# Delta-rule stage: output product one place later, norms' product at the end of the odd place, other orders on the engines

## What is computed

```python
q = _l2norm(q) * DK ** (-0.5); k = _l2norm(k)      # after a causal convolution and silu
def step(S, xs):
    q_t, k_t, v_t, g_t, b_t = xs
    S = S * jnp.exp(g_t)[..., None, None]
    kv = jnp.einsum('bhk,bhkv->bhv', k_t, S)
    S = S + jnp.einsum('bhk,bhv->bhkv', k_t, (v_t - kv) * b_t[..., None])
    o_t = jnp.einsum('bhk,bhkv->bhv', q_t, S)
    return (S, o_t)
o = o * jax.lax.rsqrt(mean(o * o) + EPS) * norm_w * jax.nn.silu(z)
return o.reshape(b_, t_, V_DIM) @ W_out
```

## Time and profile before

| | us |
|---|---|
| median of 3 runs | 2767.0 (2761.95 to 2785.57) |
| the profiled execution, its own time | 2778.46 |
| its span (first to last instruction) | 2776.8 |
| TensorE busy in the span | 2194.6 (79%) |
| VectorE busy | 1890.6 (68%) |
| ScalarE busy | 1435.8 (52%) |
| GpSimd busy | 769.1 (28%) |

### The profile page before, as it was taken

One profiled execution on the slowest core, in us unless ns is written; L12 is line 12 of the kernel. 1 busy time (PEld: TensorE's weight loads), 2 busy tenths in 40 slices (PEclk: granted clock), 3 DMA queues, 4 the chain that ended last, 5 costly groups with the idle time before them and its releaser, 6 DMA issues. The chain is left out here.

```text
span 2776.8 us, 63709 instructions
## 1 busy us (share of the span) xinstructions
PE 2194.6 (79%) x25656; PEld 1388.4 (50%) x25656; DVE 1890.6 (68%) x4429; ACT 1435.8 (52%) x2901; POOL 769.1 (28%) x845
## 2 busy tenths in 40 slices
PE   2698888889888493468888888888888886587984
PEld 1244444444444282146666666666666664365552
DVE  2477677777766325568888898888888883673433
ACT  0376667667666221255666666666666644132321
POOL 1000001000010141024444444344444442202884
PEclk8599899999887796668888988888888888597997
DMA  5000000000000042200000000000000000433334
GB/s 187 26 1 5 5 5 9 5 5 8 5 7 6 25 117 53 65 9 11 12 12 12 12 12 12 12 12 11 11 12 12 4 4 6 139 110 91 53 43 86
DMA packets 109526, 85.53 MB, mean 31 GB/s; under 512 B 22366, under 2 KB 97282, under 8 KB 108976
## 3 DMA queue, kind: packets, MB, share of 16 engines
q1 hardware_dynamic: 95664, 68.31, 8.4%
q0 software_dynamic: 13568, 13.14, 2.9%
HBM read 59.22 MB, written 22.71 MB: 30 GB/s over the span
## 5 line engine op out<-in xcount | busy, mean ns | idle before, releaser
L617 ACT ACTIVATE Pr<-Pr,nmax 128x512 f32<-128x512 f32 x512 | 341.2, 714 | 177.4 <-DVE nmax L552 175.3
L722 PE MATMUL bank<-ident,Pr 128*128 128x128 f32 x2048 | 315.5, 297 | 71.6 <-DVE PT L561 59.8
L722 PEld LDWEIGHTS bank<-ident,Pr 128*128 128x128 f32 x2048 | 242.1, 151 | 258.8 <-DVE PT L561 157.2
L552 DVE CUSTOM_DVE_ANT_0 Pr<-bank,Tb 128x512 f32<-128x512 f32 x512 | 331.0, 684 | 42.4 <-PE bank L708 42.3
L561 DVE COPY PT<-bank 128x512 f32<-128x512 f32 x256 | 176.4, 689 | 188.2 <-PE bank L736 184.0
L2431 PE MATMUL bank<-Wcv,hw 128*128 128x512 f32 x512 | 265.1, 665 | 8.8 <-POOL hw L1985 5.3
L2173 DVE TENSOR_TENSOR pr<-AC,Tc 128x30 f32<-128x30 f32 (+14 forms) x480 | 214.9, 448 | 16.9 <-POOL Tc L2049 3.6
L624 ACT ACTIVATE PT<-bank 128x512 f32<-128x512 f32 x256 | 151.0, 590 | 112.9 <-PE bank L736 83.3
L2174 DVE TENSOR_TENSOR Tc<-Tc,pr 128x30 f32<-128x30 f32 (+14 forms) x480 | 178.8, 373 | 16.5
L708 PE MATMUL bank<-kp,qp 8*128 8x512 f32 x1024 | 178.4, 696 | 1.1 <-DVE nmax L552 1.1
L2431 PEld LDWEIGHTS bank<-Wcv,hw 128*128 128x128 f32 x512 | 103.5, 214 | 125.8 <-issue 118.0
(11 more groups left out here) (398 smaller groups left out, 4533.6 us busy)
## 6 DMA issues: line engine op xcount, KB each, us to landing
aB<-alpha SPq DMA_DIRECT2D x64, 128.0 KB, 2.7
Tb<-scores SPq DMA_DIRECT2D x1, 7168.0 KB
w<-in_L_ffn_W SPq DMA_DIRECT2D x16, 256.0 KB, 5.2
rawW<-in_L_ffn_up_w SPq DMA_DIRECT2D x16, 256.0 KB, 3.1
rawW<-in_L_ffn_gw SPq DMA_DIRECT2D x16, 256.0 KB, 3.5
rawW<-in_L_ffn_down_w SPq DMA_DIRECT2D x16, 256.0 KB, 4.0
disp<-zero SPq DMA_DIRECT2D x1, 2580.0 KB, 15.5
xin<-disp SPq DMA_DIRECT2D x8, 322.5 KB, 6.3
```

What stands on the lines that cost most here:

```text
L552: V.tensor_tensor_reduce(out=Pr[:, s, i, :], in0=pS[hh][:, :], in1=Tb[:, h, at:at + L], scale=-1.0, scalar=3.0e38, op0=ALU.add, op1=ALU.mi ...
L617: A_(Pr[:, s, i, :], Pr[:, s, i, :], ACT.Exp, scale=-1.0, bias=nmax[:, s, i:i + 1])\
L722: last = TR(pT[m % 2][:, t * P:(t + 1) * P], Pr[:, (G % 2) * HG + hh, t, j * P:(j + 1) * P], ident[:, :])
```

## The change

On TensorE the output product of step k-1 moves from the end of place k to place k+1, behind the first project; the loop has one place more. The norms' product of a pair moves from the even place, behind read_out, to the end of the odd place ahead of it, behind turned. add_state(k,1) moves behind keys and gate(k,0). MISC follows. ScalarE: output one place later, behind the first project; roots from the middle of the even place to the end of the odd one; in even places weights(k,0) behind the second project. VectorE: norms(m+1) ahead of the first conv; inverse_norm right behind the second conv in both places; no substitution ahead of accumulate(k,0) in the odd place, rows 18 to 23 ahead of accumulate(k,1). GpSimd: decay(k,0) ahead of the first diag, weigh(k,0) ahead of the second. SP: the output's DMA one place later.

```diff
-            FIRST, LAST = -4, NS + 1
+            FIRST, LAST = -4, NS + 2
 (MISC)
-                if k % 2 == 0 and 0 <= k // 2 + 1 < NP:
-                    MISC += [("nm", k // 2 + 1)]
+                if 0 <= k - 2 < NS:
+                    MISC += [("out", k - 2)]
...
-                    MISC += [("ot", 2 * (k - 1)), ("ot", 2 * (k - 1) + 1), ("out", k - 1)]
+                    MISC += [("ot", 2 * (k - 1)), ("ot", 2 * (k - 1) + 1)]
+                if k % 2 == 1 and 0 <= k // 2 + 2 < NP:
+                    MISC += [("nm", k // 2 + 2)]
 (GpSimd)
                             residual(k, 1)
-                        if 0 <= m + 1 < NP and e == 0:
+                            decay(k, 0)
+                        if ahead:
                             diag(2 * (m + 1))
                         if 0 <= k < NS:
-                            decay(k, 0)
-                        if 0 <= m + 1 < NP and e == 0:
+                            weigh(k, 0)
+                        if ahead:
                             diag(2 * (m + 1) + 1)
...
 (VectorE)
+                        if ahead and e == 0:
+                            norms(m + 1)
                         if (k + 4) // 2 < NP:
                             conv(2 * (k + 4))
...
                             conv(2 * (k + 4) + 1)
+                        if past:
+                            inverse_norm(k - 1)
...
-                        if past:
-                            inverse_norm(k - 1)
-                        if ahead and e == 1:
-                            substitute(m + 1, 18, 20)
...
-                            substitute(m + 1, 20, 25)
+                            substitute(m + 1, 18, 24)
...
-                            substitute(m + 1, 25, CK - 1)
+                            substitute(m + 1, 24, CK - 1)
 (ScalarE)
                             project(2 * (k + 4))
+                        if 0 <= k - 2 < NS:
+                            output(k - 2)
                         if past:
                             square_out(k - 1, 1)
-                        if k % 2 == 0 and 0 <= k // 2 + 1 < NP:
-                            roots(k // 2 + 1)
-                        if here:
+                        if here and k % 2 == 1:
                             weights(k, 0)
                         if (k + 4) // 2 < NP:
                             project(2 * (k + 4) + 1)
+                        if here and k % 2 == 0:
+                            weights(k, 0)
...
                             turned(k - 1, 1)
-                            output(k - 1)
+                        if k % 2 == 1 and 0 <= k // 2 + 2 < NP:
+                            roots(k // 2 + 2)
 (TensorE)
                             project(2 * (k + 4))
+                        if 0 <= k - 2 < NS:
+                            output(k - 2)
                         if here:
                             read_out(k, 0)
                             read_out(k, 1)
-                        if ahead:
-                            norms(m + 1)
...
-                            add_state(k, 1)
                         if next_:
                             keys(k + 1)
                         if here:
                             gate(k, 0)
+                            add_state(k, 1)
                             gate(k, 1)
                         if past:
                             turned(k - 1, 0)
                             turned(k - 1, 1)
-                            output(k - 1)
+                        if e == 1 and 0 <= m + 2 < NP:
+                            norms(m + 2)
```

More of the change, by code:

```diff
@@ L1966, in _ @@
                             gates(k // 2 + 3)
-                        if 0 <= k - 1 < NS:
-                            output(k - 1)
+                        if 0 <= k - 2 < NS:
+                            output(k - 2)
                     sp.wait_ge(s["d_out"], 64 * NS)
@@ L2055, in _ @@
                             window(k + 1)
+                        ahead = e == 0 and 0 <= m + 1 < NP
                         if 0 <= k < NS:
@@ L2058, in _ @@
                             residual(k, 1)
-                        if 0 <= m + 1 < NP and e == 0:
+                            decay(k, 0)
+                        if ahead:
                             diag(2 * (m + 1))
                         if 0 <= k < NS:
-                            decay(k, 0)
-                        if 0 <= m + 1 < NP and e == 0:
+                            weigh(k, 0)
+                        if ahead:
                             diag(2 * (m + 1) + 1)
                         if 0 <= k < NS:
-                            weigh(k, 0)
                             weigh(k, 1)
-                        if 0 <= m + 1 < NP and e == 0:
+                        if ahead:
                             initial(m + 1)
```

## The result

| | before | after |
|---|---|---|
| median of 20 runs, us | 2775.7 (2762.0 to 2790.5) | 2762.4 (2746.2 to 2772.1) |
| ratio after to before | | 0.9944, 95% interval 0.9926 to 0.9963 |
| span of the profiled execution | 2776.8 | 2757.3 |

The kernel became 0.56% faster, 13 us by the medians and 16 by the ratio, where I had forecast 45; the size was missed by a factor of three. That the time lies in the range, and close to the 2760 us of the rival in which waits take the gain back, is in part luck: range and rivals were counted from 2767, the median of 3 runs, and 20 runs of the kernel before have their median at 2775.7. The gain itself, 1.0 us a pair by the ratio, is twice that rival's 0.5.

The account below looks back on a forecast made before the run. TensorE bounds the even place; in the odd one VectorE is fuller and TensorE waits. Terms -3.8 - 1.6 - 0.1 + 1.0 = -4.5, tempered to -3.0 a pair; fifteen pairs, 45 us: 2767 to 2722, range 2686 to 2768.

Parts of the forecast that it names:

- the rival in which waits take the gain back: Whole pair: VectorE's work, gaps and unavoidable waits come to 71 us; gain 0.5 a pair, 2760 us; chance 0.18.
- Norms at the end of the odd place: TensorE: the norms' 4.94 us leave the even place and enter the odd one, zero as work.
- Where the low clock falls: Low stretch moves from behind even-place norms to project, output and a third of read_out: 3.4 us before, 3.3 after.
- "slower" rival: Odd place: gate(k,1)'s wait and norms drop the clock before the norms; norms 6.99, read_out low; 2809 us, chance 0.07.
- Odd place, middle: TensorE from attend(k,1) to turned: add_state fills the wait for S, gate(k,1) waits about 2.1 for Kt; gain 3.8 us.
- Output a place later: TensorE, both places: project covers the 0.78 us wait for OT; gain 1.6 us a pair.
- GpSimd's order: Even place: decay no longer beside the first scan, counted at 1.21 us; otherwise 1.7 us a pair worse.
- Start and tail at zero: Before step 0 and in the tail, gives and takes counted as zero; fifteen pairs carry the gain, 45 us.
- signs named for "right": Odd place 36 to 37 us, even 31 to 33; S wait gone, norms about 4.9, first scan 1.2, VectorE's waits gone.
- named for "wrong": Norms of 7 us, read_out of 6, a pair of 71 or more, or a low stretch left mid odd place.
- the bound of 6: VectorE is idle 7.5 us in the even place, 1.9 in the odd, partly gaps; gain ends near 6 a pair.
- The rival nearest in gain: "It doesn't do what it says": bank wait holds output, VectorE's lateness the middle; 1 us a pair, 2752, chance 0.05.

Follow-up runs that it names:

- halves: Kernel after with the norms' product cut in two halves, placed in TensorE's waits for Xs and Kt in the odd place: 0.9840 of before, pair 67.2 us.
- the norms back: Kernel after with norms' product and roots back in the even place behind read_out, all else of the change kept: 0.9840 of before, pair 67.3 us.
- the dummies: Kernel after with norms back in the even place, plus unread matmuls ending the odd place: four of 128x512 0.9927, sixteen of two columns 1.0133 of before.
- the run of the three moves: Kernel before with TensorE's three moves (output later, norms and roots ending odd place, add_state between gates), no other engine orders of the change: 0.9966 of before.
- the fastest run: Kernel before with only output a place later and add_state(k,1) between the gates, norms in the even place: 0.9801 of before, median 2717.6 us.
- Filling the waits: Kernel after with unread 128x256 matmuls in odd places, three ahead of the first solve and two ahead of gate(k,1): 0.9899 of before, pair 68.4 us.
- norms alone: Kernel before with only norms' product and square roots moved to the end of the odd place: 1.0262 of before, pair 73.7 us.

## Why the prediction was wrong

*Norms at the end of the odd place: "zero as work".* This step failed. I took 4.94 us out of one place and put them into the other at the same price. The runs show two prices. In the even place TensorE has to wait for VectorE's attend anyway; the norms stood under that wait, and without them similar waits 2.7 us (after) to 4.1 us (halves). I had put that wait at 0.5 to 1, and had no low stretch behind it, where there is one of some 7 us. In the odd place they stand ahead of the read_out for which VectorE waits, 19.9 us in all between 1500 and 2200 and nothing with the norms back. Net 3.5 out, 5.3 in, 1.8 us a pair, and 29 us in all between 0.9840 and 0.9944. Three other comparisons agree in the sign: the norms' move costs 2.6% by itself, 2.2% on top of the output's and 1.65% on top of the other two moves.

*Where the low clock falls: "again nothing".* The size was given by a bound that I named and did not take. In ordinary pairs the norms ran at 3.73, better than forecast; in three odd places of 13 they ran near 6.9, the "slower" rival's mechanism, in single places. Its condition, a fall of the clock ahead of the norms, held in seven of the 13 (3, 7, 11, 15, 17, 21, 25), but in four of them the clock came back before the norms' end or start, so its price was paid in three. Against it I had held that the 2.01 us wait for Xs costs no clock. That is so in the one place I read; a low stretch stands behind that wait in 5 of the 13 odd places before and in 11 of them after. With output ahead of read_out the stretch ended soon; without it, it lasted 13 to 21 us. By the dummies the narrow form costs 4.1 us (ratios) or 1.2 us (profiled pairs) more than the wide one at the same place.

*Odd place, middle: 3.8 a pair.* Alone it is 2.6 a pair; the wait for Kt was 1.3 where I had 2.1. But in the change its gain is gone. The wait that it moves from add_state to the second gate stands right ahead of the norms. That the clock falls more often for this reason is what the places with long norms suggest (three against one); it was not shown by itself.

*Output a place later: 1.6.* Right, 1.5.

*GpSimd's order: 1.7 us less in the first scan.* Right as to the scan: all take 1.22 us. The prediction priced the long scan at 1.7 us a pair more. With the norms in the new place the run of the three moves keeps it, waits 0.7 us more for attend and is slower by 0.2%, inside both intervals. With the norms in the even place the fastest run has scans up to 2.91 us, and there the short one brought nothing.

*Start and tail at zero.* Right for the start: place 1 starts at 1272.99 against 1272.42, although read_out(0) is 8.5 us later. But fifteen pairs did not carry the gain: place 2 starts at 1308.44 against 1304.98, so the first pair's end loses 3 us, and from place 28 to the stage's end 2 us are won.

*The sum.* By terms -4.5, tempered to -3.0; it was -1.9 in the profiled execution and -1.0 by the ratio. Of the 1.1 us between the first two, 0.5 lies in the base: I took 71.5 for a pair from four pairs, and the thirteen have 71.0. With 69.1 against my 68.5 the pair itself came near, and most of the signs named for "right" were there, with norms near 7 us and a pair above 71 us, named for "wrong", in single pairs only; the gain, a small difference of two large numbers, was not. VectorE's spare time, which I used as the bound of 6, was the thing to watch: it did not shrink at all. The rival "waits take it back" had the right time from a base 9 us too low; its reason, a fuller VectorE, was wrong, since VectorE worked 2.1 us less a pair and waited for TensorE instead. The rival nearest in gain, 1 us a pair, has the output held by a bank wait; the trace has it directly behind project without one.

What stays open: why places 11, 15 and 25 and not others have the early fall that lasts (15 has it in five of the six runs with the whole norms at the end of the odd place, so there it is no accident); and how much of the 29 us is place and how much clock within the kernel after. Filling the waits gave back 12 us.

## What to carry to other kernels

Before work is moved from one place to another on the busiest engine, look at what it hides where it stands: work under a wait costs nothing, and the same work ahead of what another engine waits for costs its full length. Make the moves of a change one by one: here two gave 2.0% together, the third took 1.0 to 2.6% back, and the reordering around them gave nothing. Products of a few columns can cost more than their own length, by the low clock that follows them: here more with the small matmuls of read_out right behind them (1.0262) than with project and output between (1.0134). And take the base of a small gain from all places, not from a few.

## What the runs showed of the hardware

- At the same place, sixteen matmuls of two columns cost more than four of 512, though both take 3.6 us at the full clock: 4.1 us a place by the ratios (1.0133 and 0.9927), 1.2 by the profiled pairs (71.5 and 70.2). TensorE was busy throughout; behind or in the narrow ones the clock fell in 12 of 14 places, in or behind the wide ones in none up to the end of the next read_out.
- A low stretch begun in the norms or within 2 us behind them lasted 13 to 21 us where read_out's matmuls of 64x32 by 128 columns followed (norms alone), and mostly 3 to 7 us where project and output (128 x 128 by 256 and 128 columns) stood between.
- A scan of 128x512 on VectorE takes 1.22 us without and up to 2.91 us with GpSimd's state decay beside it.
